# A graph network kernel: its message stage without tiles found by TensorE, its attention blocks with 8 and 7 found tiles in turn

## What is computed

```
h = silu(radial @ W1 + b1); h = silu(h @ W2 + b2); w = h @ W3 + b3      # 256 weights an edge
m0 = ALPHA*(einsum(hs[src]*sh0, W00) + 1/sqrt3*einsum(hv[src], sh1, W110))
m1 = ALPHA*(einsum(hs[src], sh1, W01) + einsum(hv[src]*sh0, W10))
x  = layernorm(x + h_self(x) + segment_sum(concat(m0, m1), dst)/4)
e  = leaky_relu((x @ a_src)[src] + (x @ a_dst)[dst]); alpha = segment_softmax(e, dst)
x  = layernorm(x + segment_sum(x[src]*alpha, dst))
```

## Time and profile before

| | |
|---|---|
| median of 3 runs | 8619.93 us (8616.9 to 8624.02) |
| profiled execution | 8616.82 us, its span 8615.0 us |
| TensorE matmul, busy | 6996.6 us (81%) |
| TensorE weight load, busy | 5354.8 us (62%) |
| VectorE | 6416.2 us (74%) |
| ScalarE | 2833.3 us (33%) |
| POOL | 5314.4 us (62%) |
| mean granted clock of TensorE | 0.84 |

### The profile page before, as it was taken

One profiled execution on the slowest core, in us unless ns is written; L12 is line 12 of the kernel. 1 busy time (PEld: TensorE's weight loads), 2 busy tenths in 40 slices (PEclk: granted clock), 3 DMA queues, 4 the chain that ended last, 5 costly groups with the idle time before them and its releaser, 6 DMA issues.

```text
span 8615.0 us, 93580 instructions
## 1 busy us (share of the span) xinstructions
PE 6996.6 (81%) x26126; PEld 5354.8 (62%) x26126; DVE 6416.2 (74%) x11130; ACT 2833.3 (33%) x4982; POOL 5314.4 (62%) x5400
## 2 busy tenths in 40 slices
PE   6788888888787778888887715999999999999992
PEld 4555555555555555555555414888888888888881
DVE  7777777777777777777777734777777777777774
ACT  4444544454545445444444300111111111111110
POOL 5555555555556655555555466666666666666666
PEclk7777777777777777777777757999999999999996
DMA  2211212121212112111111211222222222222221
GB/s 61 40 39 39 41 39 40 39 41 38 40 38 41 38 39 41 39 39 31 34 33 33 48 24 35 48 52 48 49 50 47 52 47 52 48 52 47 52 48 27
DMA packets 318657, 363.23 MB, mean 42 GB/s; under 512 B 157446, under 2 KB 259510, under 8 KB 317962
## 3 DMA queue, kind: packets, MB, share of 16 engines
q0 software_dynamic: 175840, 136.07, 12.1%
q1 hardware_dynamic: 142794, 226.94, 8.4%
HBM read 251.38 MB, written 111.20 MB: 42 GB/s over the span
## 4 chain that ended last, share of the span: by engine, by line
PE 48%; issue 22%; DVE 14%; POOL 5%; DMA 5%; ACT 3%; another core or an unknown queue 2%; DVEq 0%; ACTq 0%; POOLq 0%; SPq 0%
PE tpw L661 26%; PE tpw L593 9%; DMA early<-in_x_wide,idx 5%; POOL early L476 4%; PE hid L661 4%; PE hid L583 4%; PE hid L579 3%; PE hid L602 2%; DVE prod L962 2%; DVE prod L953 2%; DVE hot L1253 1%; ACT hid L678 1%; ACT early L684 1%; POOL msgs L476 1%
## 5 line engine op out<-in xcount | busy, mean ns | idle before, releaser
L476 POOL DMA_INDIRECT early<-in_x_wide,idx x2870 | 2777.0, 968 | 2002.1 <-issue 1999.7
L476 POOL DMA_INDIRECT prod<-table,idx x2125 | 2144.8, 1009 | 1064.0 <-issue 592.8
L661 PE MATMUL tpw<-highs,hot 128*128 128x462 f32 x6125 | 2310.9, 377 | 91.7 <-DVE prod L1268 43.1
L661 PE MATMUL tpw<-lows,hot 128*128 128x462 f32 x6125 | 2291.1, 374 | 23.2 <-issue 22.1
L593 PE MATMUL tpw<-w3s,early 128*128 128x256 f32 x6252 | 2084.3, 501 | 3.1 <-DVE prod L962 3.1
L593 PEld LDWEIGHTS tpw<-w3s,early 128*128 128x128 f32 x6252 | 1545.1, 255 | 714.6 <-issue 357.9
L661 PEld LDWEIGHTS tpw<-highs,hot 128*128 128x128 f32 x6125 | 1165.3, 190 | 265.4 <-issue 60.7
L661 PEld LDWEIGHTS tpw<-lows,hot 128*128 128x128 f32 x6125 | 1158.9, 189 | 173.6 <-issue 45.7
L583 PE MATMUL hid<-hid,w2s 128*128 128x384 f32 x1042 | 559.7, 624 | 621.9 <-ACT hid L678 607.5
L684 ACT ACTIVATE early<-hid,b2s 64x384 f32<-64x384 f32 x1042 | 601.8, 578 | 1319.9 <-PE hid L583 1153.0
L579 PE MATMUL hid<-early,w1s 16*128 16x384 f32 x1044 | 663.0, 725 | 372.6 <-issue 193.1
(11 more groups left out here) (186 smaller groups left out, 8011.5 us busy)
## 6 DMA issues: line engine op xcount, KB each, us to landing
big<-qrows SPq DMA_DIRECT2D x126, 512.0 KB
scan<-prod SPq DMA_DIRECT2D x125, 425.0 KB
scan<-sums SPq DMA_DIRECT2D x130, 384.0 KB, 2.6
early<-in_x_wide,idx POOLq DMA_INDIRECT x2870
prod<-table,idx POOLq DMA_INDIRECT x2125
qbx<-qx SPq DMA_DIRECT2D x131, 128.0 KB
early<-in_radial_t SPq DMA_DIRECT2D x262, 48.0 KB
sh<-in_sh SPq DMA_DIRECT2D x131, 48.0 KB
```

Source lines behind the costliest of these rows:

```text
L476: return pool.indirect_dma_start(out=dest, out_offset=None, in_=source, in_offset=bass.IndirectOffsetOnAxis(ap=index, axis=0))
L661: mm = pe.matmul(found[i % BANKS][:, 0:BC], hot(c)[:, g, at:at + P], split(s, g), start=g == 0 and s == 0, stop=g == NBATCH - 1 and s == S ...
```

## The change

- Message stage: no tile is found any more. `find_x_slots`, `split_x`, `one_hot_x`, `find_tile`, `pick_x`, `row_x`, `mask_x` and their loads go; POOL gathers all 24 tiles.
- TensorE: layer 2 has a bank of its own (`hid[:, 1]`) and is issued for g + 2, layer 1 for g + 3.
- ScalarE: `hidden` does the second SiLU of g + 2 and at once the first SiLU of g + 3, ahead of `spread_hv`; `collect` moves from k = 0 of two iterations later to the end of k = 3 of the next one, behind `spread_hv`.
- POOL: for even k it waits as before, for odd k for layer 1 of its own group in place of layer 3 of g - 2.
- VectorE: `finish` has 16 steps in place of 9, one after each of the four operations of a slot: the scaling and the messages are cut in single components. sh is read out of `big`, whose place depends on the iteration.
- SP: `refill` loads sh first, then for each half idx (now one buffer, after the landing of the half's rows) and rad; behind it `store_sums`, as before.
- Slots of the attention tiles are worked out in iteration 0 (`find_slots`), not after the message stage.
- Attention: blocks find 8 and 7 tiles in turn and gather 17 and 18; tiles go through the five banks in turn across blocks.

The diff, cut to its core:

```
-            def gather_again(it, k, m, loads, all_tiles=False):
+            def gather_again(it, k):
                 pool.wait_ge(tpw_used, it * SLOTS + k - 1)
-                pool.wait_ge(tpw_ready, it * SLOTS + k - 1)
-                if k == 0:
-                    pool.wait_ge(idx_in[m], loads * 16 + 16)
+                if k % HALF == 0:
+                    pool.wait_ge(tpw_ready, it * SLOTS + k - 1)
+                else:
+                    pool.wait_ge(layers_done, it * SLOTS + k + 1)
+                if k % HALF == 0:
+                    pool.wait_ge(idx_in[k // HALF], it * 16 + 16)
...
-            def layer2(g):
+            def layers(g, it, k):
                 pe.wait_ge(hid_ready, g + 1)
-                pe.matmul(hid[:, 0, 0:HC], w2s[:, :], hid1[:, :], start=True, stop=True).then_inc(layer2_done, 1)
+                pe.matmul(hid[:, 1, 0:HC], w2s[:, :], hid1[:, :], start=True, stop=True)
+                layer1((it + 1) if k == SLOTS - 1 else it, (k + 1) % SLOTS)
...
+            with pe.Fori(0, ITERS) as it:
                 for k in range(SLOTS):
                     g = it * SLOTS + k
                     layer3(g, k % 2)
-                    layer2(g + 1)
-                    if finding and k % HALF == HALF - 1:
-                        find_tile(it, m, k // HALF)
-                    next_layer1(g + 2, it + 1 if k + 2 >= SLOTS else it, (k + 2) % SLOTS)
+                    layers(g + 2, it + 1 if k + 2 >= SLOTS else it, (k + 2) % SLOTS)
...
             def hidden(g, b):
-                act.wait_ge(layer2_done, g + 1)
+                act.wait_ge(layers_done, g + 2)
                 for half in range(2):
...
                 silu1().then_inc(hid_ready, 1)
...
                 for k in range(SLOTS):
                     g = it * SLOTS + k
-                    hidden(g + 1, (k + 1) % 2)
-                    if k == 0 and before is not None:
-                        collect(it - 2, m, before, CT)
+                    hidden(g + 2, k % 2)
+                    if k % HALF == HALF - 1:
+                        h = k // HALF
+                        spread_hv(it * 2 + h + 1, it + 1 if h else it, 1 - h, ahead if h else HALF)
...
+                    if k == SLOTS - 1 and before is not None:
+                        collect(it - 1, 1 - m, before, CT)
...
-            def refill(it, m, i=None):
+            def refill(it):
+                sp.wait_ge(sh_in, it * 16 + 16)
+                sp.dma_start(big[:, bass.ds(it * SHC + SHC, SHC)],
+                             sh[:, bass.ds(it * SHC + SHC, SHC)]).then_inc(sh_in, 16)
                 for h in range(2):
+                    nxt = it * (SLOTS * GT) + (SLOTS + h * HALF) * GT
                     at = it * (SLOTS * HC) + (SLOTS + h * HALF) * HC
+                    sp.wait_ge(rows_in[h], it * (16 * GT * HALF) + 16 * GT * HALF)
+                    sp.dma_start(idx[:, h * HALF:(h + 1) * HALF, :],
+                                 src[:, bass.ds(nxt, HALF * GT)]).then_inc(idx_in[h], 16)
                     sp.wait_ge(layers_done, it * SLOTS + (h + 1) * HALF)
                     sp.dma_start(rad[:, h * HALF:(h + 1) * HALF, :],
                                  radial_t[:, bass.ds(at, HALF * HC)]).then_inc(rad_in[h], 16)
...
-                if step == 0:
-                    by_sh1(it, m, tiles)
...
+                if step < 3:
+                    by_sh1(it, m, tiles, step)
+                elif step < 7:
+                    by_sh0(it, m, tiles, step - 1)
+                elif step < 11:
+                    message(it, m, tiles, step - 7)
+                elif step == 11:
                     carry_in(it, m, tiles)
                 else:
-                    scan(it, m, step - 5, tiles)
+                    scan(it, m, step - 12, tiles)
...
+FOUND = (PT, PT - 1)
+GATHERED = tuple(BT - f for f in FOUND)
+IN_PAIR = sum(FOUND)
...
-                        before = BANKS if i >= BANKS else PT if i >= PT - BANKS else PT - BANKS
-                        pe.wait_ge(found_used, b * PT + i + 1 - before + PT)
+                        pe.wait_ge(found_used, found_before(pair, k) + i + 1 - BANKS + PT)
...
-                                mm = pe.matmul(found[i % BANKS][:, 0:BC], hot(c)[:, g, at:at + P], split(s, g),
+                                mm = pe.matmul(found[(k * FOUND[0] + i) % BANKS][:, 0:BC], hot(c, k)[:, g, at:at + P],
...
-                for t in range(GT1):
-                    if t % PACE == 0 and t < GT1 - 1:
-                        pool.wait_ge(found_ready, b * PT + PT + t // PACE * 2 - LAG)
+                for t in range(GATHERED[k]):
+                    if t % PACE == 0 and t < 4 * PACE:
+                        pool.wait_ge(found_ready, found_before(pair, k) + PT + t // PACE * 2 - LAG)
```

More of the change, by code:

```diff
@@ L66 @@
 SHC = 4 * CT
[L67 to L72, removed]
+LATE = (TPAD * 4 - 2 * BLOCKS * PT - 3 * PC) // SHC
 BLOCK_STEPS = 6
@@ L594, in layer3 @@
                 mm.then_inc(tpw_ready, 1)
-            def find_tile(it, m, h):
-                pe.wait_ge(hotx_ready, it)
-                pe.wait_ge(foundx_used, it * 2 + h - 1)
-                for g in range(NBATCH):
-                    for s in range(SPLITS):
-                        mm = pe.matmul(hid[:, 1, 0:BX], hotx[m][:, g, h * P:(h + 1) * P], x_split(s, g),
-                                       start=g == 0 and s == 0, stop=g == NBATCH - 1 and s == SPLITS - 1)
-                mm.then_inc(foundx_ready, 1)
-            def iteration(it, m, finding):
+            pe.wait_ge(weights_in, 16 * 8)
+            layer1(0, 0)
+            layers(0, 0, 0)
+            layers(1, 0, 1)
+            pe.wait_ge(w3_scaled, 1)
+            with pe.Fori(0, ITERS) as it:
                 for k in range(SLOTS):
@@ L667, in _ @@
             turn(hid[:, 1, 0:1], cr[2][0:1, :], 1)
-            with pe.Fori(0, BLOCKS) as b:
-                find_rows(b)
+            with pe.Fori(0, PAIRS) as pair:
+                for k in range(2):
+                    find_rows(pair * 2 + k, pair, k)
+            find_rows(BLOCKS - 1, PAIRS, 0)
             turn(hid[0:TW, 1, 0:P], ends[:, 0, :], P)
@@ L766, in iteration @@
                     if searching:
-                        if k == 1 and first:
+                        if k == 1 and before is None:
                             act.wait_ge(base_in, 16 * 2)
@@ new lines, in message @@
+            def message(it, m, tiles, j):
+                out = msgs(m, tiles).rearrange("p (j w) t -> p j w t", j=4)
+                if j == 0:
+                    dve.wait_ge(scaled, it + 1)
+                    dve.tensor_tensor(out[:, 0, :, :], red[m][:, 0, :, 0:tiles], red[m][:, 2, :, 0:tiles], ALU.add)
+                else:
+                    ins = dve.tensor_tensor(out[:, j, :, :], tmp[:, j - 1, :, 0:tiles], red[m][:, 2 + j, :, 0:tiles],
+                                            ALU.add)
+                    if j == 3:
+                        ins.then_inc(msgs_ready, 1)
@@ L1131, in _ @@
             product_b(0, 0)
-            for step in range(9):
+            for step in range(16):
                 finish(ITERS - 1, 1, CT, step)
```

424 lines of the change are left out of this document (124 added, 300 removed).

## The result

| | before | after |
|---|---|---|
| median, us | 8618.42 (8612.29 to 8624.02, 4 runs) | 9567.55 (9564.17 to 9581.54, 4 runs) |
| message stage, us an iteration | 37.6 | 44.2 |
| attention stage, first to last matmul of a found tile, us | 3182 | 3284 |

The ratio is 1.1105, with a 95% interval of 1.1085 to 1.1124: the change makes the kernel 11% slower. About 850 us of the 949 come from the message stage (the attention stage's first matmul stands at 6110.2 in place of 5264.6) and 102 from the attention stage.

What follows compares the result with a forecast made beforehand. The prediction took a ring of waits (37.56 us an iteration) to bound the message stage and TensorE the attention stage. It summed 8616.8 + 418 (message) - 259 (attention) = 8776, said 8775 us, range 8130 to 8990.

Steps and rivals of the forecast that it cites:

- Steps 1 to 3: Message stage: landing and hv to bprod 2.2 us, VectorE's remaining work 4.75, then ScalarE's collect, ending at X + 9.1.
- X: Message stage: the end of the last gather of slot 1, from which the forecast counts its ring of waits.
- Step 4: Message stage: behind collect, ScalarE's SiLUs, then TensorE's layers 2, 1 and 3, let POOL go on at X + 19.8.
- Step 5: Message stage: rad, third load behind SP's store, lands at X + 18.2; POOL resumes at X + 25.9, ring 40.8 us.
- 1.7 + 2.15 + 3.0 = 6.85 for the three: Message stage: us for SP to issue sh, idx and rad behind the store; upper bound 9.45.
- gathers else unbroken: Message stage, expected sign: POOL has one long pause per iteration, some 10 us, and otherwise gathers without a break.
- POOL's new odd wait costs nothing: Message stage: the odd slots' wait for layer 1 of their own group, issued three groups earlier, costs nothing.
- idx with one buffer: Message stage: idx, with one buffer instead of two, lands before rad does, so POOL doesn't meet a wait.
- The attention step: Attention stage: POOL's floor 45.0 us plus half the present 3.7 loss makes 46.8 for two blocks, not 50.95; -259 us.
- SP keeps up: Message-stage rival: SP issues its loads 0.55 us apart, ring 35.1 us, kernel 8040; chance 0.32 with all up to 8600.
- The attention stage doesn't gain: Attention-stage rival: VectorE's late waits hold TensorE, two blocks stay at 50 us, kernel 8975; chance 0.08.
- The rule weighed: Attention stage: VectorE's two-port lock stops GpSimd's descriptor writes, 11.5 us in two blocks if full; rejected, 45.0 kept.

Runs made afterwards that it cites:

- e18: Changed kernel, POOL waiting for its gathers' landings only in message iterations 1 to 50 and the first 31 attention pairs; 38.4, then 44.4 us an iteration.
- e12: e5 with POOL's old wait, for layer 3 of two groups back, ahead of the odd slots; 8545.09 us, 0.9855 of the kernel before.
- e5: Changed message stage with the first half of the radial tile loaded ahead of the store, attention stage of the kernel before; 8548.74 us, ratio 0.9869.
- e16: Old message stage, changed attention stage, with 7 matmuls a found tile instead of 14; 3 us above the kernel before.
- e13: Old message stage, changed attention stage, with 17 gathers instead of 18 in the seven-tile blocks; 0 us from the kernel before.
- e17: Changed kernel with POOL waiting throughout both stages until its own earlier gathers have landed; 467 us above the kernel before, which took 8348 beside it.
- e3: Changed kernel with the first half of the radial tile loaded ahead of the store; 0.9979 of the kernel before.
- e15: Old message stage, changed attention stage, without POOL's four pacing waits per block on found tiles; 870 us above the kernel before.
- e7: Changed kernel with SP's load for every attention block cut from 1024 columns to 128; 953 us above the kernel before.

## Why the prediction was right or wrong

The direction was right and the likeliest time 793 us too low: 9568 against 8775, and outside 8130 to 8990. Of the error 430 us lie in the message stage (+850 where +418 stood) and 360 in the attention stage (+102 where -259 stood).

- *Steps 1 to 3, right.* X to bprod took 2.24 us (2.2 forecast), VectorE's rest to the last scan's end 4.73 (4.75), collect ended at X + 9.2 (9.1).
- *Step 4, right in kind, and beside the path as forecast.* Layer 2 started at X + 10.9 and was done long before rad came.
- *Step 5, the failed term.* "1.7 + 2.15 + 3.0 = 6.85 for the three" took 11.0, above the upper bound of 9.45. The landing took 1.9 (2.1), layer 3 4.7 at the low clock (5.3). So layer 3 ended and POOL went on at X + 29.5 where 25.9 stood, and 29.5 + 14.9 is the 44.4 that the trace has. The mechanism was named right, down to the 10 us of waiting in POOL and layer 1 behind a radial load; the price was wrong, since it was taken as SP's own. e18 shows that it isn't: 2.3 us with POOL's rows broken, 11.2 without. The earlier trace rows has both prices side by side, and POOL's timeline of the kernel before, had I laid it beside, shows what differs:

```profile
2028.36 0.94 POOL L476 DMA_INDIRECT early<-in_x_wide,idx  x1 [0.30 <-issue]
...
2048.42 0.96 POOL L476 DMA_INDIRECT early<-in_x_wide,idx  x1 [0.30 <-issue]
```

  The first ends a row, and POOL pauses until 2034.66; in that pause rad followed its store, after 1.68 us. The second is the twelfth gather of the row that begins at 2034.66; the steps of 2.15 and 5.6 us stand beside its last six. The change moved the burst to the end of a row of 25, the most expensive place seen here, by making that row unbroken. I had even written "gathers else unbroken" as a mark of the forecast without asking what that does to the others.
- *POOL's new odd wait costs nothing:* with the old wait back, e12's iteration is 36.7 us as e5's. *idx with one buffer:* no wait for it stands among POOL's in the changed kernel.
- *The attention step failed in kind.* "TensorE is the bound", "POOL 45.0", "half of the present loss" added. Bank waits did go, as forecast, but halving TensorE's matmuls (e16) is worth only 96 us. The number that was in front of me is 1670 gathers in 2500 us: 1.497 us each, not 1.285. I took the difference for waits on found tiles, free to vanish. After the change it is 1663 in 2500, 1.503. At 1.5 us a gather two blocks take 51 us with 34 gathers and 52.5 with 35, which is what both kernels have, and taking one gather back takes the loss back (e13). Why it is 1.5 stays open: it is 1.48 with half of the matmuls (e16) and 1.51 where POOL's waits are for landings and hardly for found tiles any more (e17), so none of the waits that the profile names makes it up alone.
- *The rivals.* "SP keeps up" didn't come true; with the radial load put early (e3, e5) the iteration took 36.7, not its 35.1. "The attention stage doesn't gain" came nearest for that stage, though two blocks took 52.7 where it said 50, and for a reason that it didn't name: the gather more, not VectorE's late waits.
- *The rule weighed.* One-hot writes beside a gather lengthen it to 1.25 or 1.28 us, as in the earlier trace rows; full exclusion isn't seen here either. The interference that decided in the message stage goes the other way: late in a row of gathers the others are delayed.

## What to carry to other kernels

Before pricing a queue's burst or an engine's floor, look at what POOL does at that moment: the same burst cost 2.3 us with POOL's rows broken and 11.2 late in an unbroken row of gathers (e18). A change that makes POOL's rows of gathers long, or moves a time-critical burst to a row's end, can have to pay for it; keep critical loads ahead of waits and out of long rows, and don't take a pacing wait for waste (e15). And a floor is total time over operations in the trace, unless it is shown that the difference can vanish.

## What was not expected of the hardware

- Beside an unbroken row of gathers the other engines' instructions can come late, matmuls from the eleventh gather of 1.25 us on: 2.1 us apart instead of 0.21, SP's records 0.7 to 1.4 instead of 0.16 (in the message stage of the kernel before already 0.65 from the seventh gather on), and perhaps VectorE's picks, up to 10 us (e15). With half of the matmuls those inside tiles weren't late in rows of up to 27 (e16). Pauses of POOL of some 2 us prevent it (e17: nearly all rows of 5 to 10 gathers, median pause 2.24 in the message stage, no matmul late by over 0.34 us).
- It isn't SP's bytes (e7). Which path the gathers and the instructions share is open. The Trainium skill, DMA: Bandwidth & Descriptors (Queues, rings and completion order), says that each DMA engine takes turns between the queues it has work for, and that one queue row belongs to the runtime, for refill among others; instruction supply behind the gathers' packets would fit, but the profile's two instruction queues hold 20 packets in the whole execution of the changed kernel, so no run here shows it.
- The kernel before took 8348 us in one execution, beside e17, and 8609 to 8669 wherever else it was measured. The record gives e17 and e18 the same chip number, 9, and beside e18 it took 8609; so the cause of the 8348 is open.
